# Scan tiles of 32 channels x 4 states in a four-layer kernel on one Trainium2 core

## The reference

```python
delta = softplus(einsum('blr,er->ble', dt, dt_proj_w) + dt_proj_b)
A = -exp(A_log)                                    # (512, 16)
dA = exp(delta[..., None] * A)                     # (b, l, e, n)
BX = delta[..., None] * Bm[:, :, None, :] * xc[..., None]
hs = scan over l of h = dA * h + BX
y = einsum('blen,bln->ble', hs, Cm) + D * xc
out = einsum('ble,de->bld', y * silu(z), out_proj_w)
```

## Time and profile before

| what | value |
|---|---|
| median of 3 runs | 3532.34 us (3526.29 to 3543.96) |
| span of the profiled execution (its own time) | 3531.4 us |
| busy: PE, POOL, DVE, ACT | 2995.4, 2784.6, 2547.8, 2415.2 us |
| the program's DMA queue | 732.89 MB, 73.9% of 16 engines' time |

### The profile page before, as it was taken

How to read it: one execution, slowest core, us unless ns; L and a number is a source line. 1 busy time by engine, 2 the same in 40 slices (tenths; PEclk the granted TensorE clock), 3 DMA queues, 4 the chain that set the end, 5 groups by cost and what they waited for, 6 DMA issues and landing times.

```text
span 3531.4 us, 58034 instructions
## 1 busy us (share of the span) xinstructions
PE 2995.4 (85%) x17392; PEld 1873.5 (53%) x17392; DVE 2547.8 (72%) x5923; ACT 2415.2 (68%) x5331; POOL 2784.6 (79%) x2583
## 2 busy tenths in 40 slices
PE   5888888888989988898898889889898998987557
PEld 3555454554655656465565646556464654654236
DVE  3356879787777768777686777867777776879870
ACT  5577778676877767677686767767676776865431
POOL 1118989888888889888898888988898888977880
PEclk9999999999999999999999999989999999998778
DMA  3017878778887888877787788878878778899981
GB/s 75 7 53 204 231 204 230 208 216 254 213 234 199 223 233 216 250 205 216 219 228 233 207 250 213 234 209 218 239 213 251 208 204 230 219 263 260 293 241 38
DMA packets 423336, 736.59 MB, mean 209 GB/s; under 512 B 53426, under 2 KB 100146, under 8 KB 423026
## 3 DMA queue, kind: packets, MB, share of 16 engines
q1 hardware_dynamic: 423026, 732.89, 73.9%
HBM read 648.84 MB, written 83.89 MB: 207 GB/s over the span
## 4 chain that ended last, share of the span: by engine, by line
PE 53%; POOL 14%; issue 9%; DVE 8%; ACT 8%; DMA 6%; SPq 2%; ACTq 0%; DVEq 0%; POOLq 0%
PE bank L483 17%; PE bank L491 7%; POOL u_rows L1523 7%; PE bank L606 6%; POOL u_rows L1516 5%; PE bank L753 5%; PE bank L687 4%; DMA w<-in_mlp_w2T 4%; PE bank L739 3%; PE bank L516 3%; PE bank L528 3%; DVE u_rows L1304 2%; ACT prob L808 2%; PE bank L544 2%; DMA u_rows<-u_dram 2%
## 5 line engine op out<-in xcount | busy, mean ns | idle before, releaser
L1523 POOL TENSOR_TENSOR u_rows<-u_rows,c_rows 128x512 f32<-128x512 f32 x1024 | 1300.9, 1274 | 173.1 <-DVE state L1309 114.7
L1516 POOL TENSOR_TENSOR u_rows<-u_rows,b_rows 128x512 f32<-128x512 f32 x960 | 1221.7, 1274 | 148.1 <-DMA u_rows<-u_dram 132.3
L979 ACT ACTIVATE bank<-d_rows,a_rep 128x512 f32<-128x512 f32 x1024 | 695.5, 688 | 271.7 <-DMA d_rows<-delta_dram 153.0
L1304 DVE TENSOR_TENSOR_SCAN u_rows<-bank,state,u_rows 128x512 f32<-128x512 f32 x512 | 642.9, 1272 | 80.9 <-ACT bank L979 64.1
L1304 DVE TENSOR_TENSOR_SCAN u_rows<-bank,u_rows 128x512 f32<-128x512 f32 x512 | 622.5, 1216 | 90.4 <-ACT bank L979 66.6
L808 ACT ACTIVATE prob<-prob,neg_max 128x256 f32<-128x256 f32 x1024 | 509.6, 504 | 17.4 <-DVE neg_max L1091 17.4
L528 PE MATMUL bank<-ident,prob 128*128 128x128 f32 x2048 | 326.6, 289 | 99.6 <-ACT prob L808 72.1
L1091 DVE CUSTOM_DVE_ANT_0 prob<-bank,band 128x256 f32<-128x256 f32 x896 | 336.1, 417 | 103.2 <-PE bank L516 68.8
L528 PEld LDWEIGHTS bank<-ident,prob 128*128 128x128 f32 x2048 | 239.9, 146 | 269.4 <-issue 214.3
L687 PE MATMUL bank<-u_rows,sum_n 128*32 128x512 f32 x2048 | 289.9, 640 | 85.5 <-POOL u_rows L1523 77.9
L516 PE MATMUL bank<-kT,q_own 32*128 32x256 f32 x2048 | 294.3, 406 | 22.1 <-DVE yg L1318 7.9
(11 more groups left out here) (170 smaller groups left out, 4920.7 us busy)
## 6 DMA issues: line engine op xcount, KB each, us to landing
u_rows<-u_dram SPq DMA_DIRECT2D x1024, 256.0 KB, 5.6
d_rows<-delta_dram SPq DMA_DIRECT2D x1024, 256.0 KB, 5.6
w<-in_W SPq DMA_DIRECT2D x28, 1024.0 KB, 8.1
zs_dram<-region_b SPq DMA_DIRECT2D x64, 256.0 KB, 4.5
xc_dram<-region_b SPq DMA_DIRECT2D x64, 256.0 KB, 3.6
u_dram<-region_b SPq DMA_DIRECT2D x64, 256.0 KB, 5.3
delta_dram<-region_b SPq DMA_DIRECT2D x64, 256.0 KB, 5.4
yg<-xc_dram SPq DMA_DIRECT2D x64, 256.0 KB, 4.1
```

What stands on the lines that cost most here:

```text
L979: e.activation(banks[at.bank][:, :], delta_of(i, k), ACT.Exp, scale=a_rep[:, j:j + 1]).then_inc(filled[at.bank], 1)
L1304: e.tensor_tensor_scan(rows, banks[at.bank][:, :], rows, state[:, k:k + 1] if i % 2 else 0.0, ALU.mult, ALU.add).then_inc(drained[at.bank], 1)
L1516: e.tensor_tensor(rows, rows, b_rows[:, :], ALU.mult).then_inc(bx_ready.sem, 1)
L1523: e.tensor_tensor(rows, rows, c_rows[:, :], ALU.mult).then_inc(hc_ready.sem, 1)
```

## The change

A scan tile becomes 32 channels x 4 states. Four tiles (a quad) share one quarter of the states; four quads cover the 16 states of a block of 128 channels. One row tile of u and of delta per 32 channels (four row tiles for a block) therefore serves four scan tiles, one in each quad of the block; these row tiles have no second buffer. Each quad loads 4 rows of B and 4 rows of C, each spread over 32 partitions, from a new DRAM buffer `bc_dram` into two alternating buffers; the matmuls and copies that spread B and C go. POOL writes the products into a new ring `h_rows` and multiplies two tiles by one instruction of 128x1024; the B and C operands repeat. The state copies take two columns at a time. The steps at which the operations stand change as the constants show. In the last two groups DVE now takes half of the C products (every second quad) where it took half of those with B; there the recurrence writes to the PSUM bank.

To make room, `x_in` shares the buffer of `z` and `aT` that of `q_own`. The residual base is formed from a second load of x, after the attention's third norm, and its bias is added within `mlp`; DVE no longer adds to `x1`. The load of the next x waits for the last `aT`. The two mask tiles become one tile of three parts, and `A_log` comes in 64 small loads of 32 partitions x 4 elements.

```diff
-SCAN0, LOAD_AT, INPUT_AT, DECAY_AT, KEEP_AT, OUT_AT, SUM_AT, GATE_AT = 10, -10, -4, -2, 1, 2, 8, 10
-GATE_LOAD_AT = 14
-SCAN_STEPS = SCAN0 + 2 * (TILES - 1) + GATE_AT + 1
+TILES, QUADS = 64, 16
+SCAN0, INPUT_AT, DECAY_AT, OUT_AT, SUM_AT, GATE_AT = 10, -6, -2, 6, 11, 14
+GATE_LOAD_AT = 20
+B_LOAD_AT, U_LOAD_AT, C_LOAD_AT = -17, -11, -5
+SCAN_STEPS = SCAN0 + 8 * (QUADS - 1) + GATE_AT + 1
 
 SCAN_PERIOD = 136
 ...
-    EL = P // NS
 ...
+    NQ = 4
+    EL = P // NQ
 ...
-        x_in = sb("x_in", [P, GT, D])
         y = sb("y", [P, GT, D])
         z = sb("z", [P, GT, D])
+        x_in = z
 ...
-        aT = sb("aT", [P, KD, G])
         q_own = sb("q_own", [P, KD, 2, G])
+        aT = q_own[:, :, 0, :]
 ...
-        D_RING, U_RING = 5, 12
-        d_rows = sb("d_rows", [P, D_RING, G])
-        u_rows = sb("u_rows", [P, U_RING, G])
-        b_rows = sb("b_rows", [P, G])
-        c_rows = sb("c_rows", [P, G])
+        H_RING = 3
+        d_rows = sb("d_rows", [P, 4, G])
+        u_rows = sb("u_rows", [P, 4, G])
+        h_rows = sb("h_rows", [P, 4 * H_RING, G])
+        b_rows = sb("b_rows", [P, 2, G])
+        c_rows = sb("c_rows", [P, 2, G])
 ...
+        bc_dram = nc.dram_tensor("bc_dram", (2, 2 * NS, G), F32, kind="Internal").ap()
 ...
             for step in range(SCAN_STEPS):
-                if step == 0:
-                    e.wait_ge(*gone(uses["middle", i, "low"]))
-                    rows_bc("b", 0)
-                if step == 7:
-                    rows_bc("c", 1)
-                k = tile_at(step, SUM_AT)
-                if k is not None and k % 4 == 3:
-                    sums(k // 4)
+                b = quad_at(step, SUM_AT)
+                if b is not None:
+                    sums(b)
 ...
+            if i:
+                e.wait_ge(*base_sum.at(i - 1))
             act_apply(e, ln_a, i, 0, x_in, y)
 ...
-            if i:
-                e.wait_ge(*aT_ready.at(i - 1, 8))
 ...
-            def keep_state(k):
-                e.wait_ge(*gone(use(f"d{k}")))
-                e.tensor_copy(state[:, k:k + 1], rows_of(i, k)[:, G - 1:G]).then_inc(state_ready.sem, 1)
 ...
+            def keep_states(b, half):
+                k = 4 * b + 2 * half
+                if not vector_out(i, b, BATCH):
+                    e.wait_ge(*gone(use(f"d{k + 1}")))
+                    e.tensor_copy(state[:, k:k + 2], half_of(i, b, half)[:, :, G - 1]).then_inc(state_ready.sem, 1)
 ...
-                if beat == AFTER - ATT0 - 2:
-                    e.wait_ge(*values_done.at(i, 8))
-                    e.tensor_tensor(x1[:, g, :, :], x_in[:, :, :], y[:, :, :], ALU.add).then_inc(base_sum.sem, 1)
-                if beat == AFTER - ATT0 - 1:
-                    e.wait_ge(*base_sum.at(i))
-                    e.tensor_tensor(x1[:, g, :, :], x1[:, g, :, :],
-                                    b2_rows[:, :].rearrange("p (o c) -> p o c", o=1).broadcast_to([P, GT, D]),
-                                    ALU.add).then_inc(base_ready.sem, 1)
                 yield
 ...
+            e.wait_ge(*x1_landed.at(i))
+            e.tensor_tensor(x1[:, g, :, :], x1[:, g, :, :], y[:, :, :], ALU.add).then_inc(base_sum.sem, 1)
 ...
+            e.wait_ge(*base_sum.at(i))
+            e.tensor_tensor(x1[:, g, :, :], x1[:, g, :, :],
+                            b2_rows[:, :].rearrange("p (o c) -> p o c", o=1).broadcast_to([P, GT, D]),
+                            ALU.add).then_inc(base_ready.sem, 1)
 ...
-            def times_b(k):
-                rows = rows_of(i, k)
-                e.wait_ge(*landed(u_landed, i * TILES + k))
-                e.tensor_tensor(rows, rows, b_rows[:, :], ALU.mult).then_inc(bx_ready.sem, 1)
 ...
+            def times_b(b, half):
+                m = b // 4
+                if half == 0:
+                    e.wait_ge(*b_landed[b % 2].at(i, b // 2 + 1))
+                    if i * QUADS + b >= H_RING:
+                        at = i * QUADS + b - H_RING
+                        e.wait_ge(*summed.at(at // QUADS, at % QUADS + 1))
+                if b % 4 == 0:
+                    for c in (2 * half, 2 * half + 1):
+                        e.wait_ge(*u_landed[c].at(i, m + 1))
+                e.tensor_tensor(half_of(i, b, half), u_rows[:, 2 * half:2 * half + 2, :], twice(b_rows[:, b % 2, :]),
+                                ALU.mult).then_inc(bx_ready.sem, 1)
 ...
+            def times_c(b, half):
+                rows = half_of(i, b, half)
+                if half == 0:
+                    e.wait_ge(*c_landed[b % 2].at(i, b // 2 + 1))
+                e.wait_ge(*gone(uses["scan", i, f"d{4 * b + 2 * half + 1}"]))
                 if i % 2 == 0:
-                    e.wait_ge(*states_kept(i, k + 1))
-                e.tensor_tensor(rows, rows, c_rows[:, :], ALU.mult).then_inc(hc_ready.sem, 1)
+                    e.wait_ge(*states_kept(i, b, half))
+                e.tensor_tensor(rows, rows, twice(c_rows[:, b % 2, :]), ALU.mult).then_inc(hc_ready.sem, 1)
 ...
+                for half in range(2):
+                    b = quad_at(step, OUT_AT + 2 * half)
+                    if b is not None and not vector_out(i, b, BATCH):
+                        times_c(b, half)
+                for half in range(2):
+                    b = quad_at(step, INPUT_AT + 2 * half)
+                    if b is not None:
+                        times_b(b, half)
 ...
-            yield from range(AFTER - 1)
+            yield from range(AFTER - 2)
+            e.wait_ge(*values_done.at(i, 8))
+            e.dma_start(x1[:, i % GROUPS, :, :], x_view[i]).then_inc(x1_landed.sem, 16)
+            yield
             if i + 1 < 2 * BATCH:
-                e.wait_ge(*base_sum.at(i))
+                e.wait_ge(*aT_ready.at(i, 8))
                 e.dma_start(x_in[:, :, :], x_view[i + 1]).then_inc(x_landed.sem, 16)
             yield
 ...
+                if m == 3:
+                    e.wait_ge(*gone(uses["middle", i, "low"]))
+                    e.dma_start(bc_dram[i % 2], dbc[RANK:RANK + 2 * NS, :]).then_inc(bc_stored.sem, 16)
 ...
-                e.dma_start(delta_of(i, k), delta_dram[i % 2, rows, :].rearrange(
-                    "(o e) t -> o e t", o=1).broadcast_to([NS, EL, G])).then_inc(
-                        d_landed[(i * TILES + k) % D_RING].sem, 16)
 ...
-                e.dma_start(rows_of(i, k), u_dram[i % 2, rows, :].rearrange(
-                    "(o e) t -> o e t", o=1).broadcast_to([NS, EL, G])).then_inc(
-                        u_landed[(i * TILES + k) % U_RING].sem, 16)
 ...
+                e.dma_start(d_rows[:, c, :], delta_dram[i % 2, rows_of(m, c), :].rearrange(
+                    "(o e) t -> o e t", o=1).broadcast_to([NQ, EL, G])).then_inc(d_landed[c].sem, 16)
 ...
+            def load_u(m, c):
+                if c == 0:
+                    e.wait_ge(*u_stored[m].at(i))
+                n = 4 * (4 * i + m) - 1
+                if n > 0:
+                    e.wait_ge(*bx_ready.at(n // QUADS, 2 * (n % QUADS) + c // 2 + 1))
+                e.dma_start(u_rows[:, c, :], u_dram[i % 2, rows_of(m, c), :].rearrange(
+                    "(o e) t -> o e t", o=1).broadcast_to([NQ, EL, G])).then_inc(u_landed[c].sem, 16)
 ...
+            def load_b(b):
+                if b == 0:
+                    e.wait_ge(*bc_stored.at(i))
+                n = i * QUADS + b - 2
+                if n >= 0:
+                    e.wait_ge(*bx_ready.at(n // QUADS, 2 * (n % QUADS) + 2))
+                e.dma_start(b_rows[:, b % 2, :], bc_dram[i % 2, b % 4 * NQ:b % 4 * NQ + NQ, :].rearrange(
+                    "n (o t) -> n o t", o=1).broadcast_to([NQ, EL, G])).then_inc(b_landed[b % 2].sem, 16)
 ...
+            def load_c(b):
+                n = i * QUADS + b - 2
+                if n >= 0:
+                    e.wait_ge(*out_formed(n // QUADS, n % QUADS))
+                at = NS + b % 4 * NQ
+                e.dma_start(c_rows[:, b % 2, :], bc_dram[i % 2, at:at + NQ, :].rearrange(
+                    "n (o t) -> n o t", o=1).broadcast_to([NQ, EL, G])).then_inc(c_landed[b % 2].sem, 16)
 ...
+                if step == 0:
+                    for c in range(2):
+                        load_u(0, c)
+                        load_delta(0, c)
+                    load_b(0)
+                    for c in range(2, 4):
+                        load_u(0, c)
+                        load_delta(0, c)
+                    load_b(1)
+                b = quad_at(step, C_LOAD_AT)
+                if b is not None:
+                    load_c(b)
+                b = quad_at(step, B_LOAD_AT)
+                if b is not None and b > 1:
+                    load_b(b)
+                for half in range(2):
+                    b = quad_at(step, U_LOAD_AT + 2 * half)
+                    if b is not None and b and b % 4 == 0:
+                        load_u(b // 4, 2 * half)
+                        load_u(b // 4, 2 * half + 1)
+                k = tile_at(step, DECAY_AT + 1)
```

(58 more changed lines are left out.)

239 lines of the change are left out of this document (85 added, 154 removed).

## The result

The changed kernel takes 3953.6 us in the median (3949.0 to 3957.5, four runs), against 3529.4 us (3526.3 to 3544.0, four runs) for the kernel before on the same chip: a ratio of 1.119, 95% interval 1.117 to 1.122. It is slower, by 424 us; 4030 us was forecast. The profiled execution spans 3955.6 us.

A forecast was written before the change was run, and what follows sets the result against it. PE set the pace before, POOL close behind; afterwards four DMA engines would. Start 275.5 us, 15 groups x 234 less 40, last scan 186 plus 8, and 94 of the rest: 4034, rounded to 4030 us; range 3560 to 4700.

The forecast's parts named there:

- Completions give the engines: Scan loads: a DMA engages no more engines than its outer count, so the new loads run on 4 of 16.
- Always the same four: Scan loads: every confined load was assumed to take the same four engines; otherwise the traffic would spread again.
- The engine's rate, 22.5 GB/s: Four busy DMA engines: each moves its 5.0 MB per group at 22.5 GB/s, taking 222 us.
- 5% idle time for the clumps: Busy engines idle between clumped u and delta loads: 5% added, making 234 us per group.
- nearly enough: Rival on DMA: four engines at 24 GB/s without idle time, 3630 us, or 3560 with slack; chance 0.15.
- deciding point: DMA: at 5.0 MB per group, engines need over 25 GB/s each to stay under 201.8 us.
- The chain of lateness: POOL's B products wait for u; C products, norms' `pow`, DVE, PE's sums and transposes then come later in turn.
- POOL's 0.13 us per pair: POOL: one 128x1024 multiply replacing two 128x512 saves 0.13 us, 129 us over 992 pairs, without surcharge for repeated operands.
- The first rival: Loads are no limit: 8.5 us less per group, 3395 us, or 3470 with shorter sums' cover; faster had chance 0.10.
- the sums' cover: PE's sums stand 3 steps after their quad's last product instead of 6: 4.5 us less cover, at worst 72 us.
- the term's other bound: PE's sums, best case: POOL's saving of 8 us per group makes up for the shorter cover.
- costed at nothing: Moved residual additions and x loads: no cost beyond bytes; without cover for the next x, 3.7 us per group.

The follow-up runs named there:

- the turned order: Changed kernel with its partitions reordered so every scan load's source has an outer count of 32 instead of 4: 3524.7 us, ratio 0.996.
- the later sums: Changed kernel with partitions reordered to outer count 32, single-column state copies and each quad's sums three steps later (SUM_AT 14, GATE_AT 16): 3452.4 us, ratio 0.976.
- SUM_AT 11: Changed kernel with partitions reordered to outer count 32 and single-column state copies, sums at the change's own step: 3520.6 us, ratio 0.996.

## Why the prediction was right

The forecast's span was 275.5 + 3470 + 194 + 94. Measured: 282.0 us to the first B product, 3396.3 to that of the last group (at 3678.3), 182.2 to the last gate (at 3860.5), 95.1 to the end. Most of the 78 us by which the forecast is high are the group's, 74 us or 4.9 per group; the last scan is 12 us high, the start 6 low. The mechanism is the predicted one. That the number came so near is partly luck, as the terms show.

- *Completions give the engines*: shown, by the completions of four kernels, by the share of 0.26, and by the time when the outer count alone is changed, in either kernel.
- *Always the same four*, which was assumed: shown by some five outstanding loads that together fill only four engines and land one by one, while a load of 16 engines issued behind such loads has twelve completions at once and four late. Which four they are, no run shows.
- *The engine's rate, 22.5 GB/s*: mis-sized. It is 25.5 GB/s in the full stretch; over the run the median row of 2 KB took 84 ns, 24.4 GB/s. That was the upper bound (24; the earlier trace rows even has a slice at 403 GB/s, 25.2 each): 5.0 MB are 205 us, not 222.
- *5% idle time for the clumps*: mis-sized the other way. 229.7 less 205 leaves 25 us, twice the 12. The times of the DMA packets agree: between the gates above, fewer than four engines are at work in 12% of the time, none in 8%. The two errors nearly cancel, which is luck. The weight was on the wrong one of them: the runs with half the loads confined, at 140 us of work per engine, still lost 102 and 280 us. The prediction's rival "nearly enough" fell for the same reason, since 24.4 GB/s was met and the group still took 230 us. Its deciding point, over 25 GB/s to stay under 201.8 us, did not decide either: against the steady 207.3 us it is 24.1 GB/s, about what the engines moved, and the kernel was slower all the same.
- *The chain of lateness* (u, POOL, `pow`, norms, PE): shown. PE's wait for the head's norm, 258.9 us, is 57.5 us in the turned order.
- *POOL's 0.13 us per pair*: consecutive starts in the changed kernel show it, 2.32 us, with no surcharge for the repeated operand:

```profile
2134.52 2.35 POOL L1513 TENSOR_TENSOR h_rows<-h_rows,c_rows 128x1024 f32<-128x1024 f32 x1 [2.64 <-DVE state L1286]
2136.84 2.34 POOL L1503 TENSOR_TENSOR h_rows<-u_rows,b_rows 128x1024 f32<-128x1024 f32 x1
```

- *The first rival's price*, 3395 or 3470 us, could be tested once the loads were spread: 3524.7 measured. The 72 us for the sums' cover are near the 68 that the later sums gave back, but by luck: the term was longer waits of PE at the sums, and from 400 to 3200 us these were 17.1 us before and 16.0 with the shorter cover (SUM_AT 11). POOL's gain had made up for it, the term's other bound; the later sums then took 14 of these 16 us, and most of the 68 is PE's busy time. The rest, 55 to 57 us, is not there. With SUM_AT 14, and over the whole run, PE's wait for the MLP weights is gone, as the rival said, and that for the reciprocals falls from 32.9 to 9.6 us. Given back are the norm at a group's head, 30.9 us before and 60.6 there, the norms' `zb`, 127.1 and 139.7, and `nb`, 4.1 and 17.5: together 56 us, about what is missing. The head's part stands where x and the residual were moved, which the prediction costed at nothing; which of the moves delays it was not tried apart and stays open.

## What to carry to other kernels

Count the engines that a load will use before counting its bytes: halving the scan's bytes cost 12% because four copies (of u and delta) or four rows (of B and C) stood outermost in the source. Turning the partition order gave all of it back. A queue share well under full, with the transfer's consumers waiting, is the sign; look at the share in a busy stretch and see whether it stands at a plain fraction such as 4 of 16. And where loads come in clumps without a second buffer, set the clump on those engines against its deadline too: with 140 us of work in a group of 207 the run with u and delta confined still lost 280 us.

## What the runs showed of the hardware

- A DMA that uses few engines holds up its issuer: issues of 0.5 us took 2.4 to 3.0 us while four engines were full, and some stores behind them in the queue landed later (`x_dram` 11.4 us, against 3.8 in the turned order).
- DVE's copy of two fp32 columns waits for a POOL multiply under way, up to 2.27 us; a copy of one column does not (155 ns at most in the turned order, with POOL busy as 135 of 240 began). The Trainium skill ("SBUF — State Buffer", section "SBUF: two separate sides") has DVE and GpSimd share a port pair that one of them holds for a whole instruction; the trace agrees for two columns, and no run shows why one column does not wait.
- PE's pauses went with longer matmuls: with 26 us less idle time at the sums, PE's work itself took 42 us less, at a mean granted clock of 0.925 against 0.917.
